# Query-side causal scores in an attention kernel: the eight diagonal blocks moved into two units of four

## The reference, cut to what matters

```python
# x: (B=32, T=1024, C=96), 6 heads of 16
k = (x @ Wk).reshape(B, H, T, hs); q = (x @ Wq).reshape(B, H, T, hs); v = (x @ Wv).reshape(B, H, T, hs)
wei = jnp.einsum('bhtd,bhsd->bhts', q, k) * C ** (-0.5)
wei = jnp.where(jnp.tril(jnp.ones((T, T), dtype=bool)), wei, -jnp.inf)
wei = jax.nn.softmax(wei, axis=-1)
out = jnp.einsum('bhts,bhsd->bhtd', wei, v).reshape(B, T, C) @ Wp + bp
```

## Time and profile before

| | |
|---|---|
| median of 3 runs | 2974.55 us (2973.9 to 2974.56) |
| the profiled execution | 2973.4 us, its span 2971.7 us |
| busy over the span | PE 2808.1 us (94%), DVE 2239.6 (75%), ACT 2043.8 (69%), POOL 1110.7 (37%) |
| query scores, L848 | 687.8 us busy, 2304 products |
| their masks, L851 | 338.7 us busy, 1536 products |
| key scores, L862 | 668.3 us busy, 3456 products |
| reductions, L956 | 1120.8 us busy, 2304 |
| exponentials, L922 | 738.4 + 208.5 us busy, 1344 + 384 |

### The profile page before, as it was taken

One profiled execution on the slowest core, in us unless ns is written; L12 is line 12 of the kernel. 1 busy time (PEld: TensorE's weight loads), 2 busy tenths in 40 slices (PEclk: granted clock), 3 DMA queues, 4 the chain that ended last, 5 costly groups with the idle time before them and its releaser, 6 DMA issues. The chain is left out here.

```text
span 2971.7 us, 85595 instructions
## 1 busy us (share of the span) xinstructions
PE 2808.1 (94%) x28966; PEld 1754.6 (59%) x28966; DVE 2239.6 (75%) x4497; ACT 2043.8 (69%) x3943; POOL 1110.7 (37%) x1969
## 2 busy tenths in 40 slices
PE   3899999999998599999999999999999998999995
PEld 2555555555554266666666666666666665555553
DVE  3576676676675488988988988888898874667675
ACT  2677777777776277777777777777777774666674
POOL 0143443443443544444444444444444421113333
PEclk9999999999999699999999999999999997999997
DMA  1113223233232576555565565555555533234445
GB/s 33 43 54 112 83 103 111 79 106 111 75 110 90 147 117 116 116 115 116 116 118 117 117 119 116 115 115 115 116 115 116 116 70 112 86 102 134 134 123 144
DMA packets 919804, 315.97 MB, mean 106 GB/s; under 512 B 848258, under 2 KB 904355, under 8 KB 919715
## 3 DMA queue, kind: packets, MB, share of 16 engines
q1 hardware_dynamic: 916258, 313.98, 44.7%
q10 hardware_dynamic: 3456, 0.79, 0.1%
HBM read 113.35 MB, written 99.88 MB: 72 GB/s over the span
## 5 line engine op out<-in xcount | busy, mean ns | idle before, releaser
L956 DVE TENSOR_REDUCE at_unit_max<-at_ps_queries 128x1 f32<-128x512 f32 (+3 forms) x2304 | 1120.8, 548 | 119.0 <-PE at_ps_queries L848 97.1
L922 ACT ACTIVATE at_probs<-at_ps_keys 128x512 f32<-128x512 f32 x1344 | 738.4, 596 | 244.4 <-PE at_ps_keys L862 216.4
L848 PE MATMUL at_ps_queries<-at_turned 96*128 96x512 bf16 (+3 forms) x2304 | 687.8, 330 | 34.0 <-DMA at_turned<-at_spread 31.7
L862 PE MATMUL at_ps_keys<-at_turned 128*128 128x128 bf16 (+3 forms) x3456 | 668.3, 275 | 2.2 <-ACT at_probs L922 2.0
L862 PEld LDWEIGHTS at_ps_keys<-at_turned 128*128 128x128 bf16 x3456 | 255.1, 97 | 240.7 <-ACT at_probs L922 122.2
L882 PE MATMUL at_ps_values<-at_probs,at_v 128*32 128x128 f32 x10752 | 373.4, 276 | 0.5 <-ACT at_probs L922 0.5
L851 PE MATMUL at_ps_queries<-mask_queries,ident_bf 128*128 128x128 bf16 x1536 | 338.7, 221 | 0.0
L816 POOL TENSOR_TENSOR at_tick<-at_one 128x1 f32<-128x1 f32 x192 | 37.1, 193 | 703.2 <-ACT at_diag_probs L922 460.5
L882 PEld LDWEIGHTS at_ps_values<-at_probs,at_v 128*32 128x32 f32 x10752 | 270.6, 109 | 42.2 <-ACT at_probs L922 1.3
L848 PEld LDWEIGHTS at_ps_queries<-at_turned 96*128 96x128 bf16 x2304 | 217.5, 98 | 100.9 <-DMA at_turned<-at_spread 33.3
L922 ACT ACTIVATE at_diag_probs<-at_ps_keys 128x512 f32<-128x512 f32 x384 | 208.5, 595 | 12.7 <-PE at_ps_keys L862 4.3
(11 more groups left out here) (207 smaller groups left out, 5095.8 us busy)
## 6 DMA issues: line engine op xcount, KB each, us to landing
qkv_rows<-cb_packed SPq DMA_DIRECT2D x32, 1536.0 KB, 8.1
at_stacks<-qkv_rows SPq DMA_DIRECT2D x192, 256.0 KB, 3.2
cb_x<-in_x_dram SPq DMA_DIRECT2D x32, 384.0 KB, 3.6
cb_x_again<-in_x_dram SPq DMA_DIRECT2D x32, 384.0 KB, 4.6
x_after_conv<-cb_x SPq DMA_DIRECT2D x32, 384.0 KB, 5.0
attention_rows<-at_att SPq DMA_DIRECT2D x384, 32.0 KB, 2.2
ff_att_rows<-attention_rows SPq DMA_DIRECT2D x32, 384.0 KB, 3.7
ff_x<-x_after_conv SPq DMA_DIRECT2D x32, 384.0 KB, 4.7
```

What stands on the lines that cost most here:

```text
L848: mm = pe.matmul(pq[:, u % QBANKS, 0:n], QT[0:STACK, slot, qb * P:(qb + 1) * P], KT[0:STACK, slot, k0:k0 + n], start=True, stop=True)
L862: mm = pe.matmul(pk[:, bank_k, c0:c0 + n * P], KT[:, slot, kb * P:(kb + 1) * P], QT[:, slot, q0 * P:(q0 + n) * P], start=(c0 == 0), stop=True,
L922: act.activation(probs, pk[:, (slot * NU + k) % KBANKS, :], ACT.Exp, scale=scale).then_inc(S["probs"], 1)
L956: dve.tensor_reduce(MX[:, r % 2, qb, k0 // BANK:k0 // BANK + 1], pq[:, u % QBANKS, 0:n], AX.X, ALU.max).then_inc(S["unit_max"], 1)
```

## The change

The mask tile grows to 128 x 512 and holds the same 128 x 128 triangle four times. The query units are laid out anew: ten units hold only blocks below the diagonal, and two more, at the end of the list, hold four diagonal blocks each, as four products of 128 columns side by side in one bank, followed by one mask product over all 512 columns. VectorE reduces such a unit to four maxima in one instruction, and they go to a third column of `MX`. The list has 12 units as before; `QSTEP`, `NQ` and the rest of the order stay.

```diff
-    w["mask_queries"] = sb("mask_queries", [P, P], BF16)
+    w["mask_queries"] = sb("mask_queries", [P, BANK], BF16)
...
-                link(pool.affine_select(out=w["mask_queries"][:, :], in_=w["mask_queries"][:, :],
-                                        compare_op=ALU.is_ge, fill=NEG, base=0, pattern=[[-1, P]],
-                                        channel_multiplier=1), 6)
+                blocks = w["mask_queries"][:, :].rearrange("p (t n) -> p t n", n=P)
+                link(pool.affine_select(out=blocks, in_=blocks,
+                                        compare_op=ALU.is_ge, fill=NEG, base=0,
+                                        pattern=[[0, BANK // P], [-1, P]], channel_multiplier=1), 6)
...
-    QUNITS = [(qb, k0, min(BANK, (qb + 1) * P - k0)) for qb in range(TILES)
-              for k0 in range(0, (qb + 1) * P, BANK)]
+    QUNITS = [[(qb, k0, min(BANK, qb * P - k0))] for qb in range(TILES) for k0 in range(0, qb * P, BANK)]
+    QUNITS += [[(qb, qb * P, P) for qb in range(g, g + BANK // P)] for g in range(0, TILES, BANK // P)]
...
-        MX = sb("unit_max", [P, 2, TILES, 2])
+        MX = sb("unit_max", [P, 2, TILES, 3])
...
                 def query_scores(h, r, lap, u):
...
-                    mm = pe.matmul(pq[:, u % QBANKS, 0:n], QT[0:STACK, slot, qb * P:(qb + 1) * P],
-                                   KT[0:STACK, slot, k0:k0 + n], start=True, stop=True)
-                    if k0 + n == (qb + 1) * P:
-                        mm = pe.matmul(pq[:, u % QBANKS, n - P:n], w["ident_bf"][:, :], w["mask_queries"][:, :],
+                    c0 = 0
+                    for qb, k0, n in QUNITS[u]:
+                        mm = pe.matmul(pq[:, u % QBANKS, c0:c0 + n], QT[0:STACK, slot, qb * P:(qb + 1) * P],
+                                       KT[0:STACK, slot, k0:k0 + n], start=(c0 == 0), stop=True, skip_group_check=True)
+                        c0 += n
+                    if len(QUNITS[u]) > 1:
+                        mm = pe.matmul(pq[:, u % QBANKS, :], w["ident_bf"][:, :], w["mask_queries"][:, :],
                                        start=False, stop=True, skip_group_check=True)
                     mm.then_inc(S["q_scores"], 1)
...
-                            dve.tensor_reduce(MX[:, r % 2, qb, k0 // BANK:k0 // BANK + 1], pq[:, u % QBANKS, 0:n], AX.X,
-                                              ALU.max).then_inc(S["unit_max"], 1)
+                            qb, k0, n = blocks[0]
+                            if len(blocks) > 1:
+                                peaks, scores = MX[:, r % 2, qb:qb + len(blocks), 2], pq[:, u % QBANKS, :].rearrange(
+                                    "p (t n) -> p t n", n=P)
+                            else:
+                                peaks, scores = MX[:, r % 2, qb, k0 // BANK:k0 // BANK + 1], pq[:, u % QBANKS, 0:n]
+                            dve.tensor_reduce(peaks, scores, AX.X, ALU.max).then_inc(S["unit_max"], 1)
```

More of the change, by code:

```diff
@@ L843, in query_scores @@
                     slot = (r - 2) % SLOTS
-                    qb, k0, n = QUNITS[u]
                     if u == 0:
@@ L944, in body @@
                 def body(i, r, lap, on):
-                    for u, (qb, k0, n) in enumerate(QUNITS):
+                    for u, blocks in enumerate(QUNITS):
                         if u == OUT_QUNIT and on(5):
```

## The result

The changed kernel takes 3011.41 us (median of 4, 3009.7 to 3012.45) against 2974.56 us: a ratio of 1.0122, 95% interval 1.0105 to 1.014, +37 us. Forecast were 3000.5 us and a range of 2984 to 3020. The sign, the place of the loss and most of its size were right; one stretch of the ring was put down to the wrong engine, and 11 us of the 37 were not foreseen.

A forecast was written before the change was run, and what follows sets the result against it. ScalarE and TensorE were taken to pace each head in turn; +0.28 - 0.04 - 0.06 = +0.18 us a head, -0.07 at the loop's jump, gave +26 us and 3000.5 us, range 2984 to 3020.

The forecast's parts named there:

- the ring: One attention head's period, 7.32 us: ScalarE up to k5, TensorE to k7, ScalarE to k1, TensorE to the output-sum copy.
- Same work, other place: Whole head: the same 20 products and 5632 columns before and after; 896 mask columns move next to k5 and k6.
- second rival: Whole kernel, no difference: time added after k4 is given back before k1, 0.165 us earlier; 2977 us; chance 0.08.
- first rival: Diagonal units u10 and u11: weight loads bind, 97 ns a product instead of 55; +90 us, 3064; chance 0.07.
- First half, +0.28: k4 to the values: diagonal units u10 and u11 take 0.44 us each, so the values start 0.28 later.
- Second half, -0.04 and -0.06: k7 to the output-sum copy: k1 0.04 us earlier, limited by k8's exponential; u5 without its mask saves 0.06.
- TensorE from k1 to the copy: Last stretch of a head: TensorE's work sets the time, so dropping u5's mask saves 0.06 us.
- The two heads after the turn: The two heads following the one where the loop jumps back: forecast like plain heads, 7.50 us each.
- The turn: One head in six, loop jumps back: 0.34 us idle before u0 disappears behind work; 7.61 becomes 7.54.
- The sum: All heads together: 156 at +0.18 us and 31 with the loop's jump at -0.07, giving +26 us.
- third rival: Values held by ScalarE: later k5 and k6 cost nothing, saved masks stay as gain; 2947 to 2956 us; chance 0.09.

## Why the prediction was right, and where not

**Same work, other place: right.** Both lists hold the same products, and the time follows the columns between k4 and k7 (128-column masks, other places). The second rival, no difference, falls with the result: +37 us, since k7 to k1 shrank by 0.05 us and not by the 0.165 that it needs. The trace has four 128-column products in 0.22 us, so weight loads do not bind either, as the first rival had it. The Trainium skill ("TensorE: Matmul & The Clock Gate", "Back-to-back issue gap") has 81 ns for each in such a stream; here they took 55.

**First half, +0.28: right.** Measured +0.27 from the copy to k7's exponential (4.23 to 4.50).

**Second half, -0.04 and -0.06: sum near by luck, reasons wrong.** From k7's exponential to the copy the plain head gains 0.07, not 0.10. k1 did come 0.05 earlier after k7, as forecast, but that is not what moved the copy. All of the gain comes from the masks before k0 (TensorE reached k0 late before; now k7's exponential releases it, at 1535.20, 0.05 after the 0.6 us from 1534.55 are over). u5's mask gave nothing, as its own run shows. The failed step is "TensorE from k1 to the copy": the issue of a transfer on ScalarE, 0.62 us, stood there, and I had read ScalarE's timeline only up to the exponentials. With it moved to SyncE a head of the changed kernel takes 7.29 instead of 7.52.

**The two heads after the turn: missed, +0.09 each** (7.596 against 7.506, before the table's rounding). ScalarE's lag of 0.08 us existed before as well. It cost 0.01 (7.33 against 7.32), because TensorE's masks made k0 that late anyway. Taking the masks away uncovered it. The trace before shows the heads of 7.33 next to those of 7.32; I took only one head.

**The turn: hidden on TensorE, as forecast, and +0.11 mostly on ScalarE.** u0 starts 0.22 after k6 at the turn, like in any head, and k7 comes 0.02 later than in a plain one:

```profile
1502.16 0.38 PE L865 MATMUL at_ps_keys<-at_turned 128*128 128x384 bf16 x2
1502.38 0.22 PE L850 MATMUL at_ps_queries<-at_turned 96*128 96x128 bf16 x1
```

The head still costs 7.65 and not 7.54 (the prediction wanted it within 0.1 of the plain 7.50), since k7's exponential starts 0.53 us after its products and not 0.43, the same lag with a longer operation (57 ns) at L45; with the waits in the other order it costs 7.54. ScalarE's own jump is over 1.3 us before that exponential. In the kernel before the turn had cost 0.29 more than a plain head: 0.25 on TensorE and 0.10 of this lag, less 0.06 that the masks before k0 cost a plain head and not this one. The forecast took off the 0.25 and kept the remaining 0.04 without naming the lag.

**The sum.** Per six heads 1.19 us were lost and 0.83 forecast: 3 x 0.02 in plain heads, 2 x 0.09 after the turn, 0.11 at it, together 0.35. Times 187 / 6 that is 11 us, the whole of the miss.

**The third rival** (ScalarE holds the values) fell: the values moved by 0.27 with TensorE's stream.

## What to carry to other kernels

Count columns and instructions before and after, then ask between which two waits they stand: in a ring that two engines pace in turn, moving the same work across a wait is a change of time by itself. Read every row of an engine that is on the path, its DMA issues among them, before calling another engine the bound of a stretch. And read more than one iteration: the odd ones show a lag that something on the path covers, and the change may take that cover away.

## What the runs showed of the hardware that was not expected

- Issuing one small transfer (2 x 1024 bf16) kept ScalarE from its next instruction for 0.62 us. Moved to SyncE, it gave 24 us in the kernel before and 41 us in the changed one, and nothing in the plain heads of the layout with the diagonal units ahead of k4.
- Two waits ahead of one ScalarE instruction are not symmetric: with the late one first, the instruction started 0.08 us later in two heads of six and 0.10 at the turn, because the queue computed the second wait's value (35 ns) only after the first was met; with the late one last it started as fast as elsewhere.
- The jump of a hardware loop is not a fixed price. On TensorE it cost 0.25 us a turn in the kernel before and 0.02 in the changed one, where the engine reaches u0 0.33 us later while its queue jumps at the same time. The branch starts 2.10 us after the copy in the one, 2.09 in the other, and is listed at 0.21 us. In the kernel before, u0's load follows 0.48 us after the branch's start. With the diagonal units ahead of k4 it does so too, but there k4's exponential, which lets k6 through, ends 0.24 us later, so the branch starts at 2.34: 0.46 us of idle time, and a turn that costs 0.54 more than a plain head.
